# Thirteen steps in other places of the engines' orders, squares without a wait between them, and a normalisation that reads with jumps where it wrote with jumps

## What is computed

```python
x = x + tanh(g_xattn) * mlstm(layernorm(x), ctx, ctx)      # q = layernorm(x), k = v = ctx
x = x + tanh(g_ffn) * ffn(layernorm(x))

# mlstm, for each sequence, 8 heads of 32 features:
ig, fg = gates of concat(q, k, v)                # two small matrix products
cs = cumsum(log_sigmoid(fg))
log_D = where(causal, cs[:, None] - cs[None, :], -inf) + ig[None, :]
D = exp(log_D - max(log_D))
C = (q_h @ k_h.T / sqrt(32)) * D
h = (C / (max(abs(sum(C)), exp(-max(log_D))) + eps)) @ v_h
out = layernorm(h) * ln_scale

# ffn: 1024 hidden features
y = square(relu(x @ W_fc.T)) @ W_proj.T
out = number of spikes of 5 leaky integrate-and-fire steps on y, / 5
```

## Time and profile before

| | |
|---|---|
| median of 3 runs | 661.75 us (658.73 to 664.57) |
| the profiled execution's own time | 662.98 us |
| its span | 661.2 us |
| busy in it: PE | 589.5 us |
| DVE | 542.4 us |
| POOL | 485.6 us |
| ACT | 484.4 us |

### The profile page before, as it was taken

One profiled execution on the slowest core, in us unless ns is written; L12 is line 12 of the kernel. 1 busy time (PEld: TensorE's weight loads), 2 busy tenths in 40 slices (PEclk: granted clock), 3 DMA queues, 4 the chain that ended last, 5 costly groups with the idle time before them and its releaser, 6 DMA issues.

```text
span 661.2 us, 17665 instructions
## 1 busy us (share of the span) xinstructions
PE 589.5 (89%) x6032; PEld 483.9 (73%) x6032; DVE 542.4 (82%) x1222; ACT 484.4 (73%) x1011; POOL 485.6 (73%) x531
## 2 busy tenths in 40 slices
PE   1265887799999999999999999999999999999795
PEld 0155776778787878787788878787878777787684
DVE  4878787889989998899989998999888998958522
ACT  4555777678787888788878878788878867676463
POOL 6157678867996969787897799787969788675232
PEclk9996799999999999999999999999999999999898
DMA  8915553845276335916573538642680556300000
GB/s 262 225 52 115 97 115 70 176 83 96 83 156 169 74 91 147 208 26 139 115 186 60 96 110 155 159 86 80 150 207 18 97 101 148 63 2 33 1 33 32
DMA packets 73192, 71.33 MB, mean 108 GB/s; under 512 B 8720, under 2 KB 68752, under 8 KB 73104
## 3 DMA queue, kind: packets, MB, share of 16 engines
q1 hardware_dynamic: 71888, 70.00, 47.3%
q10 hardware_dynamic: 1216, 0.21, 0.2%
HBM read 27.44 MB, written 8.39 MB: 54 GB/s over the span
## 4 chain that ended last, share of the span: by engine, by line
PE 51%; DVE 10%; issue 10%; ACT 7%; POOL 7%; SPq 4%; DMA 2%; POOLq 0%; ACTq 0%; DVEq 0%
PE z_ps L997 16%; PE y_ps L1057 16%; PE arg_ps L702 3%; PE qk_ps L717 3%; POOL sq_lo L1040 3%; DVE spikes L1075 3%; PE misc_ps L463 2%; SPq L650 2%; PE misc_ps L529 2%; SPq L513 2%; ACT sq_hi L1019 1%; POOL c_lo L746 1%; PE pv_ps L766 1%; PE pv_ps L764 1%; PE pv_ps L841 1%
## 5 line engine op out<-in xcount | busy, mean ns | idle before, releaser
L1040 POOL TENSOR_TENSOR sq_lo<-w_raw,sq_hi 128x512 fp32r<-128x512 f32 (+1 forms) x96 | 113.0, 1178 | 66.2 <-ACT w_raw L1020 66.1
L746 POOL TENSOR_TENSOR c_lo<-decay 128x512 bf16<-128x512 f32 x128 | 132.5, 1042 | 22.4 <-DVE decay L736 22.2
L997 PE MATMUL z_ps<-x_hi,wfc_hi 128*128 128x512 f32 (+1 forms) x288 | 115.7, 402 | 5.9 <-ACT w_raw L1007 4.1
L1057 PE MATMUL y_ps<-sq_hi,wpr_hi 128*128 128x512 f32 (+1 forms) x288 | 115.1, 400 | 1.1 <-POOL sq_lo L1040 1.1
L997 PE MATMUL z_ps<-x_hi,wfc_lo 128*128 128x512 f32 (+1 forms) x288 | 107.2, 372 | 0.0
L997 PE MATMUL z_ps<-x_lo,wfc_hi 128*128 128x512 f32 (+1 forms) x288 | 107.2, 372 | 0.0
L1057 PE MATMUL y_ps<-sq_lo,wpr_hi 128*128 128x512 f32 (+1 forms) x288 | 106.8, 371 | 0.0
L1057 PE MATMUL y_ps<-sq_hi,wpr_lo 128*128 128x512 f32 (+1 forms) x288 | 106.6, 370 | 0.0
L736 DVE TENSOR_TENSOR decay<-qk_ps,decay 128x512 f32<-128x512 f32 x128 | 87.1, 680 | 18.5 <-PE qk_ps L717 14.4
L728 ACT ACTIVATE decay<-arg_ps,lqk_col 128x512 f32<-128x512 f32 x128 | 86.5, 676 | 19.7 <-PE arg_ps L705 19.1
L1040 POOL TENSOR_TENSOR sq_lo<-relu,sq_hi 128x512 fp32r<-128x512 f32 (+1 forms) x48 | 56.3, 1173 | 37.9 <-ACT relu L1020 35.2
(11 more groups left out here) (139 smaller groups left out, 1686.2 us busy)
## 6 DMA issues: line engine op xcount, KB each, us to landing
x_in<-x SPq DMA_DIRECT2D x32, 256.0 KB, 3.5
kT_in<-ctx_cols SPq DMA_DIRECT2D x32, 256.0 KB, 3.8
v_in<-ctx_rows SPq DMA_DIRECT2D x32, 256.0 KB, 3.2
k_stack<-kT_hi SPq DMA_DIRECT2D x64, 128.0 KB, 3.4
k_stack<-kT_lo SPq DMA_DIRECT2D x64, 128.0 KB, 3.7
q_stack<-qT_hi SPq DMA_DIRECT2D x64, 128.0 KB, 4.0
q_stack<-qT_lo SPq DMA_DIRECT2D x64, 128.0 KB, 4.2
out<-w_raw SPq DMA_DIRECT2D x32, 256.0 KB, 3.6
```

The source lines that it names most:

```text
L746: e.tensor_tensor(c_lo[i % NCH][:, :], c, top(c), ALU.subtract).then_inc(sem("c_lo"), 1)
L997: ins = e.matmul(z_ps[:, tokens(q)], lhsT, rhs, start=(n == 0), stop=(n == len(terms) - 1))
L1040: e.tensor_tensor(sq_lo[n % NSQ][:, tokens(q)], relu[n % NRE][:, tokens(q)], sq_hi[n % NSQ][:, tokens(q)].bitcast(fp32), ALU.subtract).the ...
L1057: ins = e.matmul(y[:, c, :], w[:, j, c * P:(c + 1) * P], h, start=(j == 0 and i == 0 and (c == 0 or whole)), stop=(j == FT - 1 and i == 2) ...
```

## The change

Three edits.

1. `ln1_apply` walks the 256 features of a token in another order. Before, the instruction read x in a row and wrote `xln` 4 numbers (16 bytes) apart. Now it writes `xln` in a row and reads x 32 numbers (128 bytes) apart. The same numbers land in the same places.
2. `square` no longer passes its first instruction through `link`: the second `Square` follows without a wait. In place of 144 pairs with a wait there are 144 without.
3. Thirteen steps stand elsewhere in the lists: one on SP, three on ACT, seven on PE (one of them in the loop), and two on POOL, where `k_weigh(5)` and `v_lo_step(5)` change places. DVE's list is the same.

```diff
             for t in range(ST):
-                ins = e.activation(xln[b % NXL][:, t, :].rearrange("p (c d g) -> p c g d", c=DC, g=HPC),
-                                   x_in[b % NX][:, t, :].rearrange("p (c g d) -> p c g d", c=DC, g=HPC),
+                ins = e.activation(xln[b % NXL][:, t, :].rearrange("p (c d g) -> p c d g", c=DC, g=HPC),
+                                   x_in[b % NX][:, t, :].rearrange("p (c g d) -> p c d g", c=DC, g=HPC),
                                    ACT.Identity, bias=off[:, t:t + 1], scale=rstd[:, t:t + 1])
...
-            link(e, "scalar", e.activation(sq_hi[n % NSQ][:, tokens(q)], r, ACT.Square))
+            e.activation(sq_hi[n % NSQ][:, tokens(q)], r, ACT.Square)
             e.activation(r, r, ACT.Square).then_inc(sem("square"), 1)
...
             load_x(e, 4)
+            stack_heads(e, 0)
             load_x(e, 5)
-            stack_heads(e, 0)
...
-            q_hi(e, 3)
             decay_exp(e, 0, 0)
+            q_hi(e, 3)
             ln1_apply(e, 4)
...
+            ln2_rstd(e, 3)
             square(e, 1, 4)
-            ln2_rstd(e, 3)
...
             state(e, 1)
-            pv(e, 1, 0)
             arg(e, 1, 3)
...
             arg(e, 2, 1)
+            pv(e, 1, 0)
             qk(e, 2, 0)
...
+            z_step(e, 0, 4)
             state(e, 2)
-            z_step(e, 0, 4)
...
+            inter(e, 2)
             pv(e, 2, 0)
-            inter(e, 2)
...
+            z_step(e, 1, 5)
             y_step(e, 1, 2)
...
                 z_step(e, 2 * n, 4)
+                gate_products(e, 4 * n + 6)
                 arg(e, 4 * n + 3, 0)
-                gate_products(e, 4 * n + 6)
```

More of the change, by code:

```diff
@@ L1211, in scalar_program @@
             am_split(e, 1, 2)
+            decay_exp(e, 0, 0)
             q_hi(e, 3)
-            decay_exp(e, 0, 0)
             ln1_apply(e, 4)
@@ L1304, in scalar_program @@
             ln3_rstd(e, 3)
-            q_hi(e, 9)
             relu_step(e, 1, 5)
@@ L1308, in scalar_program @@
             ln3_apply(e, 3)
+            q_hi(e, 9)
             square(e, 1, 5)
@@ L1675, in tensor_program @@
             pv(e, 3, 0)
+            y_step(e, 1, 0)
             x2_T(e, 2)
-            y_step(e, 1, 0)
             pv(e, 3, 1)
@@ L1694, in tensor_program @@
             arg(e, 5, 1)
-            z_step(e, 1, 5)
             state(e, 4)
@@ L1701, in tensor_program @@
             pv(e, 4, 1)
-            qk(e, 5, 1)
             y_step(e, 1, 3)
             z_step(e, 1, 6)
+            qk(e, 5, 1)
             arg(e, 5, 2)
@@ L1893, in gpsimd_program @@
             square_lo(e, 1, 3)
-            v_lo_step(e, 5)
+            k_weigh(e, 5)
             v_hi_step(e, 6)
@@ L1897, in gpsimd_program @@
             k_lo(e, 9)
-            k_weigh(e, 5)
+            v_lo_step(e, 5)
             k_weigh_lo(e, 5)
```

## The result

| | before | after |
|---|---|---|
| median of 7 runs, us | 661.75 (658.73 to 664.57) | 667.67 (665.68 to 670.24) |
| ratio, 95% interval | | 1.0099 [1.0076, 1.0123] |
| span of the profiled execution, us | 661.2 | 665.8 |
| 140 to 600 us of it: PE's matmuls, PE idle | 4590, 4.9 us | 4518, 8.2 us |

The account below looks back on a forecast made before the run. The prediction took PE's own work to bound the middle (140 to 600 us) and chains of single steps the ends. Its terms, -0.7 - 0.5 - 0.5 - 0.8 = -2.5 us, took 661.75 to 659.3 us, range 653 to 664.

Parts of the forecast that it names:

- Part 1: First normalisation, x read with jumps: 595 ns each instead of 828; two pairs at the front give -0.7 us.
- Rival A: First normalisation: reads with jumps cost what the writes did, near 828 ns; 660.0 us, chance 0.20.
- Part 2: Squares without a wait: 0.12 us saved a pair, four pairs on the path, -0.5 us, ends 0 and -4.7.
- Part 3: Middle, 140 to 600 us: freed ACT time -0.5 us; gate products moved ahead of `arg` 0, other end +1.2.
- The last warning of the prediction: Middle: if it got shorter by more than PE's idle 4.9 us, PE's busy time would hide waits.
- The -0.5 us for freed ACT time in the middle: 140 to 600 us: freed ACT time reaches PE only through PE's waits, 3.3 us together; taken as -0.5, end -4.9.
- Part 4: The moves in the prologue, summed: -0.8 us, ends -3 and +1.5.
- the +1 of `load_x(5)`: Prologue: x5, issued 6 us later behind the transfers of `stack_heads(0)`, may reach DVE late; 0, other end +1 us.
- (a): Prologue, ACT: `decay_exp(0, 0)` ahead of `q_hi(3)` starts 1.3 us earlier, most given back at DVE; -0.3 us.
- (b): Prologue, PE: `pv(1, 0)` moved to just ahead of `qk(2, 0)`; later steps get up to 1.6 us; -0.5 us.
- C: Slower: a read jump costs more than a write jump and ACT's later steps come later; about 664 us, chance 0.12.
- Rival B: Prologue carries its moves whole and PE leaves its half clock sooner: about -7.7 us, 654 us, chance 0.18.

Follow-up runs that it names:

- e1: Kernel before, with only the first normalisation changed to read x with jumps and write `xln` in a row: 662.11 us, ratio 1.0006.
- e2: Kernel before, with only the wait between the two squares of every pair taken out: 664.89 us, ratio 1.0053.
- e5: Kernel before without the wait between squares, except that squares (2n, 6) and (2n, 7) of each loop turn keep it: 660.30 us, ratio 0.9980.
- e3: Kernel before, with only `gate_products(4n+6)` moved ahead of `arg(4n+3, 0)` on PE in the loop: 665.25 us, ratio 1.0057.
- e4: Kernel before, with only the twelve moves of steps outside the loop (SP, ACT, PE, POOL): 661.75 us, ratio 1.0004.
- e12: The changed kernel with the wait put back for squares (2n, 6) and (2n, 7) alone: 664.53 us, ratio 1.0032 to the kernel before.
- e10: Kernel before with 32 more small matmuls in PE's idle time near 23 us, the control of e9: 662.61 us, ratio 1.0015.
- e9: Kernel of e3 with 32 more small matmuls in PE's idle time near 23 us: 663.71 us, ratio 1.0030 to the kernel before.

## Why the prediction was wrong

It said 659.3 us, 653 to 664; the time was 667.67, outside the range and on the other side of no change. By its own steps:

**Part 1**, "I take 595 ns, as the pair of rows is nearest to that", failed. DVE's rows on 16 columns in PSUM say nothing of ACT's SBUF reads; the read with 128-byte jumps takes 846 ns, 18 more than the 16-byte write jumps. The second of a pair now starts 0.74 us after the first (before 0.64: 9.59 and 10.23), so the pair takes 1.56 us and not the 1.09 of the prediction:

```profile
8.97 1.56 ACT L415 ACTIVATE xln<-x_in,off,rstd 128x256 f32<-128x256 f32 x2 [0.23 <-DVE off L374]
```

Rival A had it, and the rule on lines of 16 bytes that the prediction set beside it (the Trainium skill, Advanced Engine Details and Errata, SBUF Cachelines) agrees with the measurement. The term was -0.7, and e1 measured +0.06% with ±0.2%: nothing. The first gate products did come at 16.52 instead of 16.92, but that is no sign for the term: e2, which leaves the reads alone, has them at 16.19, and from the start of the second pair to them it is 4.23 us in the changed kernel and 4.12 before.

**Part 2** had its price right: 0.12 us a pair, second square 0.52 to 0.53 us after the first, ACT down by 13.5 us in the middle in e2. It had the effect wrong, by sign. The step that failed is that what is "taken from an engine that already has room" is worth nothing in the middle: room on ACT bounds a gain from above, but no loss from below. The work that ACT releases starts earlier too, and the first is POOL's `sq_lo`, 0.1 us earlier into a DVE instruction that it keeps out. A term of -0.5 with ends 0 and -4.7 had to have an end above zero; e2 measured +3.5 us (0.53% of 661). That the edit is worth having shows in e5, -1.3 us, more than the -0.5 of the term.

**Part 3**, "Without `arg` between them the margin is 0.14 us", compared the end of DVE's record with the start of PE's as if the one released the other at once. The trace of before already has the hand-over between these two steps at 0.26 us, so the other end, +1.2 us, was what had to be taken; the five holes measure 1.4. The rest of e3's 0.57% (3.8 us), above all two late loads that held up the second gate products by 1 us each, no step had. The last warning of the prediction, that PE's busy time may hide waits, was right, with the wrong sign: the share went from 0.989 to 0.982, while the number of matmuls fell by 1.6%. The -0.5 us for freed ACT time in the middle no run measures by itself.

**Part 4** and its -0.8: e4 measured 1.0004 ± 0.002. A term of this size can't be told from zero here; the +1 of `load_x(5)` or the gains of (a) and (b) may each be there. The interval is -1.0 to +1.6 us and holds 0 and -0.8 alike, and no run parts the moves.

**The rivals.** The slower one, C, was built on a dearer read jump and got 0.12 and 664 us. Its sentence "A late `q_lo` ... would add 1.2" named one part of the true mechanism, as an aside. The chance of slower by over 1%, 0.07, stood on the belief that the middle of the kernel had no term above 1.2 us; it had two of 3.5 and 3.8. Rival B's own terms add up to 8.5 us (2.9, 1.9, 1, 1.7 and 1), not 7.7, so it stood at 653 us. Its gain from the clock gets no support: e3, whose prologue is that of before, was granted 0.99 of the clock in the first 140 us, not 0.91, and had issued 1088 matmuls by then, not 1133.

One thing adds to the after profile alone. Behind its 0.83 us wait for `q_lo`, which was over at 444.71, PE's granted clock fell for 3.4 us (the windows 445 to 449 and 449 to 456 us, columns as in the earlier trace rows):

```profile
445.00:449.00 4.00, 4.00 (x34) 2.97 (x31) 3.27 (x11) 0.79 (x2) 2.95 (x3) 0.57 1.17 155
449.00:456.00 7.00, 7.00 (x34) 5.53 (x33) 5.99 (x12) 6.62 (x15) 2.16 (x2) 1.00 0.13 30
```

0.57 is mostly the lower of the two levels, 1.2 of 2.4 GHz, in a stretch where PE was busy throughout. 3.4 us at half speed would cost 1.7 us; set beside before, PE fell back by 1.5 from 444.7 to 448.8. e3 had two such waits (0.83 and 0.85 us) and e12 one (0.81), and both kept their clock there, so this is not a part of the loss of every run.

## What to carry to other kernels

An engine with room to spare is no licence to move its work: what it releases starts earlier as well, and two engines that exclude each other (here DVE and POOL on SBUF) can turn 0.1 us into a microsecond on one of them, and here 0.4 to 0.6 us on PE, in every turn of a loop, so look at who starts first where their rows are within 0.1 us (or a few tenths, as at L374), and give such an edit an end above zero. A margin between one engine's end and another's start counts only beyond the hand-over, which other rows of the same two steps show. It differs from step to step on the same engines: 0.26 us here from `q_lo` to the gate products, 0.10 from `x_lo` to `z_step`. When an edit costs more than its place explains, run it alone, then put back the one instance that stands before the suspected collision: that can keep the gain and drop the loss, as e5 did.

## What was not expected of the hardware

- ACT, 128x256 f32 in SBUF: 592 ns with both sides in a row, 828 with the output 16 bytes apart, 846 with the input 128 bytes apart. The reads cost more than the 18 ns between the last two: the second of a pair starts 0.72 to 0.74 us after the first, not 0.63 or 0.64.
- A DVE instruction of 2 numbers a partition (L374) takes 0.13 to 0.15 us at its shortest and up to 2.04 us beside POOL; in e2 it was kept out over the end of one POOL instruction and through the whole next one.
- Where a 16 KB packet of instructions starts 0.9 to 1.2 us after a 256 KB load of x is issued, at the two loads above, it lands in 3.7 to 4.4 us and not in 2.6 to 2.9 (eight of 28 cases, without exception).
- Thirty-two small matmuls in idle time, with no effect of their own that e10 could tell (1.0015, interval from 0.9993), moved which loads are hit in the profile; e9 measured 1.0030 where e3 had 1.0057, with intervals that overlap.
